# The last two steps of a grouped attention, rebuilt on all five engines

## What is computed

```
q = rmsnorm(x_norm @ Wq)            # 32 heads of 128, 4 per group
k, v = rmsnorm(ctx @ Wk), ctx @ Wv  # 8 groups, 512 keys
attn = softmax(q k^T / sqrt(128) + mask)
x = x + concat(attn @ v) @ Wo
...
# seventh sublayer: for each row of 512, which 154 (TOPK) entries of ctx are largest
# (the channels that get the one or the other gate)
```

## Time and profile before

| | us |
|---|---|
| median of 3 executions (871.33 to 874.70) | 874.07 |
| span of the profiled execution | 875.2 |
| busy in it: TensorE, VectorE, ScalarE, GpSimd | 783.4, 719.1, 519.3, 428.5 |
| steps 12 and 13 (645.6 to 678.3, 678.3 to 711.5) | 32.7, 33.2 |
| step 14 (711.5 to 742.9) | 31.4 |
| step 15 up to its last turn (742.9 to 777.0) | 34.1 |
| from there to the tail (777.0 to 793.5) | 16.5 |

### The profile page before, as it was taken

One profiled execution on the slowest core, in us unless ns is written; L12 is line 12 of the kernel. 1 busy time (PEld: TensorE's weight loads), 2 busy tenths in 40 slices (PEclk: granted clock), 3 DMA queues, 4 the chain that ended last, 5 costly groups with the idle time before them and its releaser, 6 DMA issues. The chain is left out here.

```text
span 875.2 us, 16429 instructions
## 1 busy us (share of the span) xinstructions
PE 783.4 (90%) x5146; PEld 634.7 (73%) x5146; DVE 719.1 (82%) x1732; ACT 519.3 (59%) x1408; POOL 428.5 (49%) x380
## 2 busy tenths in 40 slices
PE   1976899858987999999999999999999999578878
PEld 0474676534776898898898897898898898465446
DVE  7878998968788888888888888887887887955974
ACT  6864898747466756756656756756656656321421
POOL 3237087805226647646646746646646746531110
PEclk9999999979999999999999999999999999789899
DMA  8253246562203102102102202201200300103001
GB/s 304 93 193 121 75 150 207 163 187 80 96 2 97 50 26 95 50 24 96 48 24 80 64 24 74 70 24 52 92 24 28 116 24 25 48 25 117 1 0 49
DMA packets 39114, 68.23 MB, mean 78 GB/s; under 512 B 5729, under 2 KB 18593, under 8 KB 38946
## 3 DMA queue, kind: packets, MB, share of 16 engines
q1 hardware_dynamic: 39074, 67.73, 23.5%
HBM read 62.38 MB, written 5.34 MB: 77 GB/s over the span
## 5 line engine op out<-in xcount | busy, mean ns | idle before, releaser
L1966 ACT ACTIVATE layer_attention_probs<-xnT,stats 128x512 f32<-128x512 f32 x128 | 93.9, 734 | 137.8 <-DVE stats L2075 137.8
L2244 DVE TENSOR_SCALAR_CACHE_REDUCE xn<-ctxT,candidate 128x512 bf16<-128x512 f32 x240 | 168.8, 741 | 0.0
L1750 PE MATMUL bank<-layer_attention_keysT,layer_attention_queriesT 128*128 128x512 f32 x384 | 122.6, 428 | 5.0 <-DVE layer_attention_queriesT L2068 5.0
L2087 DVE TENSOR_TENSOR layer_attention_probsT<-bank,layer_attention_probsT 128x512 fp32r<-128x512 f32 x128 | 88.0, 688 | 39.8 <-ACT layer_attention_probsT L1974 38.3
L1750 PEld LDWEIGHTS bank<-layer_attention_probsT,layer_attention_values 128*128 128x128 f32 x768 | 99.7, 191 | 23.0 <-DVE layer_attention_probsT L2087 9.3
L1750 PE MATMUL bank<-layer_attention_probsT,layer_attention_values 128*128 128x256 f32 x768 | 103.4, 284 | 14.0 <-DVE layer_attention_probsT L2087 13.9
L1750 PE MATMUL bank<-layer_attention_wo,layer_attention_headsT 128*128 128x512 f32 x384 | 104.5, 417 | 3.0 <-issue 3.0
L1974 ACT CAST layer_attention_probsT<-bank 128x512 fp32r<-128x512 f32 x128 | 74.7, 584 | 50.4 <-PE bank L1826 50.1
L1696 POOL TENSOR_TENSOR layer_attention_mixed<-layer_attention_mixed,xnT 128x512 f32<-128x512 f32 x32 | 52.1, 1627 | 86.3 <-DMA xnT<-inverse_sums 82.8
L1750 PE MATMUL bank<-layer_attention_l_wq,layer_attention_xnT 128*128 128x512 f32 x384 | 93.5, 392 | 0.0
L1750 PE MATMUL bank<-layer_attention_l_wkv,layer_context_parts 128*128 128x256 f32 x720 | 90.5, 278 | 0.0
(11 more groups left out here) (322 smaller groups left out, 1673.0 us busy)
## 6 DMA issues: line engine op xcount, KB each, us to landing
layer_attention_l_raw_qo<-in_wqT SPq DMA_DIRECT2D x9, 1024.0 KB, 5.1
xnT<-inverse_sums SPq DMA_DIRECT2D x16, 512.0 KB, 3.7
layer_attention_l_raw_qo<-in_woT SPq DMA_DIRECT2D x8, 1024.0 KB, 7.1
tw_raw<-in_w_gateT SPq DMA_DIRECT2D x8, 688.0 KB, 5.2
tw_raw<-in_w_upT SPq DMA_DIRECT2D x8, 688.0 KB, 4.2
tw_raw<-in_w_downT SPq DMA_DIRECT2D x6, 768.0 KB, 4.7
layer_attention_l_raw_kv<-in_wkvT SPq DMA_DIRECT2D x9, 512.0 KB, 4.8
ternary<-tw_rounded SPq DMA_DIRECT2D x8, 344.0 KB, 2.6
```

Of the source, the lines that this page charges most:

```text
L1750: last = pe.matmul(out, stationary[f][a], moving[f][b], start=f == 0 and x == 0, stop=f == count - 1 and x == 2)
L1966: a.activation(probs[:, u % 3, :], masked[:, u % 2, :], ACT.Exp, bias=negmax[:, u:u + 1], scale=-1.0, accum_out=sums[:, u:u + 1]).then_inc ...
L2087: v.tensor_tensor(probsT[:, 1, p % 2, :, columns], T[u % 2][:, :].rearrange("p (c q) -> p c q", c=CPB), probsT[:, 0, p % 2, :, columns], A ...
L2244: own(k.nc.vector.tensor_scalar((k.flags if flags is None else flags)[:, r % 2], row_tile(k.ctxT, r), k.candidate[:, r:r + 1].bitcast(F32) ...
```

## The change

The last two steps, 14 (`LATE`) and 15, get lists of their own.

- Search: the last four counts move from step 14 to steps 12 and 13, two more in each (`DOUBLED`: units 1 and 4 have two). Step 14 then has 12 of the 20 pieces, step 15 has 8 (`PIECES_AT`).
- Last weights: the redundant loads of a ninth group are gone, arrays included. SyncE loads the last group's output weights at the end of step 13; in step 14 ScalarE casts them where it cast query weights, into the query weights' buffer, free by then, and GpSimd makes the low part after its work of step 14. The key, value and query weight splits of step 14 are gone.
- Probabilities: in steps 14 and 15 VectorE inverts each unit's sum by itself, at the end of the unit before (`invert_unit`), and ScalarE multiplies the probabilities with it (`scale_probs`) ahead of the turn. The round through DRAM and GpSimd's multiplication are gone there; GpSimd only splits the heads.
- Last products: the output projection of step 14 moves to units 1, 3 and 5 of step 15. That of step 15 goes by head (`last_out`): head 0 before the last mix, then heads 1, 2 and 3. GpSimd splits heads 0 to 2, ScalarE and VectorE the last one, straight from PSUM. The banks are R and J[0].

The loops are one round shorter, and the two steps more are written out.

```diff
     SCALE = HD ** -0.5
     KEYS = TPB
     TURNS = (KEYS, 0, 1)
-    CHOICE = {STEPS - 2: (0,), STEPS - 1: (2, 4, 6)}
+    LATE = STEPS - 2
     OWN_START, OWN_STEP = BISECT_PER_ROUND - 2 * FRONT_COUNTS, 2 * BISECT_PER_ROUND
-    OWN_AT = {x: OWN_START + OWN_STEP * x for x in (0, 1, 2, STEPS - 3, STEPS - 2)}
-    OWN_AT[STEPS - 1] = OWN_AT[STEPS - 2] + BISECT_PER_ROUND + CHOICE_COUNT
-    OWN_END = OWN_AT[STEPS - 1] + 3 * CHOICE_COUNT
+    EVEN, DOUBLED = (1,) * UNITS, (1, 2, 1, 1, 2, 1, 1, 1)
+    PIECES_AT = {LATE: (2, 1, 2, 1, 2, 1, 2, 1), LATE + 1: (1,) * UNITS}
     with ExitStack() as s:
...
-                with sp.Fori(0, STEPS // 2 - 1) as i:
+                with sp.Fori(0, STEPS // 2 - 2) as i:
                     run((i, 1))
                     run((i, 2))
-                run((None, STEPS - 1), last=True)
-                sp.wait_ge(gw.q_loaded, 16 * (GROUPS + 1))
-                sp.wait_ge(gw.kv_loaded, 16 * (GROUPS + 1))
+                run((None, LATE - 1), loads=False)
+                sp.wait_ge(S_["o_low"], 2 * (GROUPS - 1))
+                load_o(GROUPS - 1)
...
+                def split_heads(step, j):
+                    heads = slice(2 * j, 2 * j + 2)
+                    g.wait_ge(S_["mix_copied"], at(step, PAIRS, 2 * j + 2))
+                    g.wait_ge(S_["out_added"], added(after(step, -1), TPB))
+                    g.tensor_copy(headsT[:, 0, heads, :], mixed[:, heads, :]).then_inc(S_["heads_high"], 1)
+                    g.wait_ge(S_["heads_high"], at(step, 2, j + 1))
+                    g.tensor_tensor(headsT[:, 1, heads, :], mixed[:, heads, :], headsT[:, 0, heads, :], ALU.subtract)\
+                     .then_inc(S_["heads_low"], 1)
+
+                def split_last(step, h):
+                    g.wait_ge(S_["mix_copied"], at(step, PAIRS, h + 1))
+                    g.wait_ge(S_["out_psum"], at(step, TPB, 0))
+                    g.tensor_copy(headsT[:, 0, h, :], mixed[:, h, :]).then_inc(S_["last_high"], 1)
+                    g.wait_ge(S_["last_high"], h + 1)
+                    g.tensor_tensor(headsT[:, 1, h, :], mixed[:, h, :], headsT[:, 0, h, :], ALU.subtract)\
+                     .then_inc(S_["last_low"], 1)
+
...
+                run((None, LATE - 1))
+                run((None, LATE), weights=False)
+                for half in range(2):
+                    o_weights_low(GROUPS - 1, late_wo, half)
                 for j in range(2):
-                    scale_heads((None, STEPS - 1), j)
+                    split_heads((None, LATE), j)
+                for h in range(REP - 1):
+                    split_last((None, LATE + 1), h)
 
             @block.tensor
...
-                    pe.wait_ge(S_["exp_ready"], at(step, UNITS, u + 1))
+                    if late(step):
+                        pe.wait_ge(S_["probs_scaled"], late_unit(step, u))
+                    else:
+                        pe.wait_ge(S_["exp_ready"], at(step, UNITS, u + 1))
...
+                def last_out(t, h):
+                    if t == 0 and h == 0:
+                        pe.wait_ge(S_["rowsT_low"], at(final, CHUNKS, CHUNKS))
+                    if t == 1 and h == 0:
+                        pe.wait_ge(S_["out_added"], added(after(final, -1), 1))
+                    if t == 0 and h < REP - 1:
+                        pe.wait_ge(S_["last_low"], h + 1)
+                    if t == 0 and h == REP - 1:
+                        pe.wait_ge(S_["final_low"], 1)
+                    for x, (a, b) in enumerate(PARTS):
+                        last = pe.matmul(final_bank(t)[:, :], headsT[:, a, h, t * P:(t + 1) * P], late_wo[:, b, h, :],
+                                         start=h == 0 and x == 0, stop=h == REP - 1 and x == 2)
+                    if h == REP - 1:
+                        last.then_inc(S_["final_psum"], 1)
+
+                def run_last(step):
+                    before = after(step, -1)
+                    for u in range(UNITS):
+                        if u == 1:
+                            project_out(before, 0, 0)
+                        if u == 3:
+                            project_out(before, 0, 1)
+                        if u == 5:
+                            project_out(before, 1, 0)
+                            project_out(before, 1, 1)
+                        turn_probs(step, u)
+                        if u + 2 < UNITS:
+                            scores(step, u + 2)
+                        if u == 0:
+                            mix(before, PAIRS - 1)
+                        if u in (2, 4, 6):
+                            mix(step, u // 2 - 1)
+                    for t in range(TPB):
+                        last_out(t, 0)
+                    mix(step, PAIRS - 1)
+                    for h in range(1, REP):
+                        for t in range(TPB):
+                            last_out(t, h)
...
+                def late_weights_high(half):
+                    if half == 0:
+                        a.wait_ge(S_["o_loaded"], 16 * GROUPS)
+                        a.wait_ge(S_["q_psum"], at(final, TPB, TPB))
+                    heads = slice(half * REP // 2, (half + 1) * REP // 2)
+                    last = a.copy(late_wo[:, 0, heads], raw_o[:, heads])
+                    if half == 1:
+                        last.then_inc(S_["o_high"], 1)
+
+                def scale_probs(step, u):
+                    a.wait_ge(S_["unit_inverse"], late_unit(step, u))
+                    a.activation(probs[:, u % 3, :], probs[:, u % 3, :], ACT.Copy,
+                                 scale=late_inverse[:, step[1] - LATE, u:u + 1]).then_inc(S_["probs_scaled"], 1)
...
+                        ahead, at_u = (step, u + 1) if u + 1 < UNITS else (following, 0)
+                        exponentials(ahead, at_u)
+                        probsT_high(step, u)
+                        if late(ahead):
+                            scale_probs(ahead, at_u)
+                        if odd and u == 1:
+                            o_weights_high(step)
+                        if not odd and not late(step) and u == 4:
+                            kv_weights_high(group(step) + 1)
+                        if not odd and not late(step) and u in (5, 6):
+                            q_weights_high(group(step) + 1, u - 5)
+                        if late(step) and u in (5, 6):
...
+                def run_last(step):
+                    before = after(step, -1)
+                    for u in range(UNITS):
+                        if u == 1:
+                            copy_mixed(before, PAIRS - 1)
+                        if u in (3, 5, 7):
+                            copy_mixed(step, u // 2 - 1)
                         if u + 1 < UNITS:
                             exponentials(step, u + 1)
-                        elif not last:
-                            exponentials(following, 0)
                         probsT_high(step, u)
-                        if odd and u == 1:
-                            o_weights_high(step)
-                        if not odd and u == 4:
-                            kv_weights_high(group(step) + 1)
-                        if not odd and u in (5, 6):
-                            q_weights_high(group(step) + 1, u - 5)
+                        if u + 1 < UNITS:
+                            scale_probs(step, u + 1)
+                    a.wait_ge(S_["mix_psum"], at(step, PAIRS, PAIRS))
+                    a.wait_ge(S_["out_psum"], at(step, TPB, 0))
+                    a.copy(headsT[:, 0, REP - 1, :], V[:, 0:SEQ]).then_inc(S_["final_high"], 1)
...
+                def invert_unit(step, u):
+                    v.wait_ge(S_["exp_ready"], at(step, UNITS, u + 1))
+                    v.reciprocal(late_inverse[:, step[1] - LATE, u:u + 1], sums[:, u:u + 1]).then_inc(S_["unit_inverse"], 1)
+
+                def search(own, counts, pair=0):
+                    for j in range(pair, pair + counts):
+                        bisection_count(k, own, j % 4)
+                        if j % 4 == 3:
+                            bisection_update(k, own)
+                    return (pair + counts) % 4
+
+                def choose(own, units):
+                    for _ in range(units):
+                        choose_piece(k, own, *next(pieces))
+
+                pieces = iter([(r, piece) for r in range(0, CTILES, 2) for piece in range(CHOICE_PIECES)])
+
...
+                        if late(step):
+                            choose(own, PIECES_AT[step[1]][u])
+                        else:
+                            pair = search(own, counts[u], pair)
+                        if late(ahead):
+                            invert_unit(ahead, at_u)
+                    if not first:
+                        add_out(before, 1)
+                    return pair
...
+                def run_last(step, own):
+                    before = after(step, -1)
+                    for u in range(UNITS):
                         if u + 1 < UNITS:
```

(48 more changed lines are left out.)

165 lines of the change are left out of this document (79 added, 86 removed).

## The result

The changed kernel takes 864.58 us (median of 4 executions, 859.2 to 865.53) where the kernel before takes 873.12 (4 executions, 871.33 to 874.70): a ratio of 0.9886, 95% interval 0.9853 to 0.9919. The profiled execution took 865.53, its span is 863.6.

> The changed kernel itself once more, so that the runs beside it have it on the same chip. If the first comparison was right its ratio is near 0.989, and the stages come out as before: step 14 about 36.9 us, step 15 23.4, the end 8.7.

A forecast was written before the change was run, and what follows sets the result against it. TensorE was taken to bound up to step 14, VectorE step 15, then a serial end. Turn (15,0) +7.0, step 15 -9.9 and the end -7.1 gave -10.0: 864 us, range 861 to 867.5, eight in ten 860 to 870.

The forecast's parts named there:

- steps 12 and 13: Two more counts in each step, taken by VectorE's idle time: 0; a reciprocal in step 13's last unit adds 0.6 us.
- Turn (15,0): First turn of step 15, behind late weights, held piece 1, reciprocal and scaling: at 749.9 instead of 742.88, +7.0 us.
- The first rival: Nothing held at (14,7) or in step 15's first units: turn (15,0) 2.5 earlier, step 15 2.3 shorter, 859 us; chance 0.14.
- Waits of step 14: TensorE waits twice in step 14: about 0.95 us at turn 2 and 0.7 in unit 6.
- Turn (14,7): Turn of step 14's last unit: near 744.1 instead of 741.7, 2.4 us later, bounds 0 and 5.5.
- Step 15: First to last turn of step 15, with 8 pieces instead of 15: 24.3 us where it was 34.15, -9.9.
- What was held: In the old step 15, VectorE time lost waiting on GpSimd's instructions, beside 15 us for 15 pieces; given no size.
- The end: Last turn to last add, without GpSimd's multiplications and the two DMAs: 8.8 us instead of 15.9, -7.1.
- The scaling: ScalarE's scaling of the probabilities in steps 14 and 15: 0.69 us each, 16 of them 11 us.
- The second rival: Some four of 16 reciprocals held at 1 us each, or step 15 takes 28 at low clock: 868.5 us; chance 0.17.
- the third: At the end, products by head wait for GpSimd's splits or run at 1.2 GHz; end 12 to 13, 868 us; chance 0.07.
- the fourth: In step 14 TensorE stands some 3 us at a time and the clock falls; from three gaps slower, 879 us; chance 0.07.

The follow-up runs named there:

- halves_early: Changed kernel, but GpSimd starts each half of the late weights' low parts once ScalarE has rounded it, and unit 5 of step 14 gets unit 6's second piece: 859.82 us.
- halves_early_inv: halves_early, but in unit 1 of step 14 VectorE inverts the next unit's sums ahead of its two choice pieces: 859.49 us, 859.01 when run again.

## Why the prediction was right, step by step

- **Sum.** Forecast -10.0 in span; the profiled pair gave -11.6, the stretch -11.27. Each term was near: +0.70 in steps 12 and 13 (0.6), +5.53 in step 14 (6.4, the 7.0 less the 0.6), -10.74 in step 15 (-9.9), -7.20 at the end (-7.1). The two larger errors, 0.9 in step 14 and 0.8 in step 15, both made the kernel faster than forecast. The border's +0.44 was not seen coming. That the median came out at 864.58 for 864.0 is in part luck: it fell by 8.54, from 873.12, where the forecast took 10.1 from 874.07, and the four executions spread from 859.2 to 865.53.
- **Turn (15,0)** was forecast for 749.9 and came at 749.67, through the chain that was laid out: late weights, held piece 1, reciprocal, scaling, turn. Of that time 0.56 is the later start of step 12; counted from there the turn is 6.23 later than before, not 7.0. The moving of that piece and the early halves, which shortened the seam by 1.95 and 2.86, show that the hold was the cause. The first rival, at 859, had no hold at the seam nor in the first units of step 15, and both were there. halves_early, without the first, takes 859.82, but that does not confirm the price: it has the other hold, and its stretch is only 1.40 shorter.
- **Waits of step 14.** 0.95 at turn 2 was 1.14, with the cause named (a scan taking turns with the heads' split; the inverse put ahead of it removes the wait). The 0.7 in unit 6 was 0.33: the scores start 0.69 after turn (14,6) instead of 0.36. Turn (14,7) came at 744.66 instead of 744.1, all of it the later start.
- **Step 15** was 23.41 for 24.3. The mis-sized term is unit 1, and the path through it was another one: turn 2 came 7.50 after turn 0 and not 8.2. The forecast had VectorE's queue set it, with piece 3 held for 1.8 by the heads' split. But piece 3 took 0.87, between the two halves of that split, and turn 2 came by ScalarE, which waited for turn 1 before its cast and scaling; turn 1, at the low clock (0.57) as feared, came 5.51 after turn 0:

```profile
753.77 0.87 DVE L2410 SCALAR_TENSOR_TENSOR ctxT<-ctxT,left 128x256 f32<-128x256 f32 x2
...
755.82 0.58 ACT L2042 CAST layer_attention_probsT<-bank 128x512 fp32r<-128x512 f32 x1 [0.75 <-PE bank L1860]
...
757.17 0.63 PE L1860 MATMUL bank<-ident,layer_attention_probs 128*128 128x128 f32 x4 [0.69 <-ACT layer_attention_probs L2077]
```

So that this term is off by only 0.7 is luck. In halves_early, at full clock and with piece 3 held (2.26), the forecast's path does set that turn, 7.35 after turn 0. The later intervals were 3.97, 1.98, 5.36, 1.99 and 2.61 for 4.1, 1.9, 5.5, 1.9 and 2.7.
- **What the step was credited to** was partly wrong. Fewer pieces stood as the first reason; putting the seven back costs 1.67 in step 15 and 1.16 at the end, not the 7 us that they last. "What was held", named beside them without a price, was some 6 us by the trace of the kernel before. Undone alone, the search gives 2.98 of the 11.27 in the stretch (1.35 of it in step 13, where an update met a multiplication), the order by head 1.20, the moved projection 1.20; the rest is not split further by these runs.
- **The end**: 8.69 for 8.8, its 18 products at 0.242 each for 0.244.
- **The scaling** took 0.72 for the 0.69 taken, the reciprocal 0.156 for 0.16. The second rival (reciprocals held, or the clock low for longer) did not come; nor did the third, an end of 12 to 13; nor the fourth, TensorE standing for 3 us at a time in step 14: besides the seam, no turn of that step waited over 1.14, and its clock was 1.00.

**A version that beats both kernels** is halves_early_inv: 0.9845 (0.9826 to 0.9865) where the changed kernel beside it has 0.9905 (0.9883 to 0.9926), and 0.9863 (0.9832 to 0.9894) once more, without the changed kernel beside it.

## What to carry to other kernels

A division that is moved ahead is paid for where something waits for it: here at six of sixteen turns and, through ScalarE's queue, at the scores behind a query cast. So ask which of them has slack and what stands ahead of the reciprocal in its queue. Where two engines hold each other instruction by instruction, start the long one earlier (1.40 us here); moving the held one by a unit, even with one that isn't held in its place, only found the next neighbour (+0.35). Undoing one part at a time showed that the parts' shares were not where the sum had put them, although the sum was right.
